# Six attentions on one core: the order of stages in six kinds of loop, and where SP issues the fold matrices

## The chip, the cores and the metric

The kernel runs on one core of one Trainium2 chip. The metric is the device time of one launch in microseconds (us), as the median of several runs. One more view, the profile, shows a single execution, instruction by instruction.

## The reference

Four transformer layers run one after another on `x` of shape (8, 512, 256), with a context of the same shape. Together they hold six attentions with 16 heads of 16 columns, and three feed-forward networks of width 1024:

```python
x = L0(x, ctx)   # attention 0: 64 wide causal window with slopes on x; attention 1: full, on ctx; FFN 0 (gelu)
x = L1(x, ctx)   # attention 2: causal on x, attention 3: full on ctx, both behind doubled projections; FFN 1 (gelu)
x = L2(x, ctx)   # attention 4: full, on the normalized ctx; FFN 2 (silu)
x = L3(x, ctx)   # attention 5: full, on ctx; layer norm
# each attention: softmax(q k^T * scale) v, then the output matrix, a residual and (mostly) a layer norm
```

## The kernel before

**Loops.** `LOOPS` (L110) lists 48 loops, one for each of 8 batch rows `b` and 6 attentions `a`. Batch rows go in pairs, and inside a pair the two rows alternate: (0,0), (1,0), (0,1), (1,1) and so on to (0,5), (1,5), then (2,0). `LOOP_NO` numbers them.

**Streams.** While one loop's attention runs, the tail of the loop before (output matrix, norms, feed-forward) and the start of the loop after (projections, first maxima) run beside it. `streams(j)` (L237) makes the lists: stream 0 is the attention's own 16 steps (`scores`, `values`, `sums`, `heads`, and `load` of the second half of the packed queries and keys), stream 1 its row maxima from head 6 on, stream 2 the work between, stream 3 what needs the context or a prefetched input. The first loop has a stream 4: `fold_stages` multiplies the doubled projections of attentions 2 and 3 into single matrices (six products in two halves, `fold`, with a `fold_bias` for each), then asks for later weights (`first_weights`) and makes five bias rows.

**The written order.** `MERGE` (L251) holds a string of digits for each kind of loop. Each digit takes the next stage from the stream of that number. The key is `first`, `last`, or the attention followed by the parity of the batch row. `plan()` walks the strings, and every engine goes through the resulting `PLAN` in the same order, doing its own share of each stage. An engine that waits therefore holds up everything behind it in the plan.

**How an attention's operands travel.** `project` makes q and k on TensorE (PE). ScalarE (ACT) writes the high bf16 part (L793), VectorE (DVE) the rest (L901), `middle` makes the middle part on ACT (L798) and the low part on GpSimd (POOL, L1027). SyncE (SP) sends each part to DRAM (L521) and, in `load`, fetches them back in the packed layout, twelve transfers of 128 KB for each half (L549). The `scores` matmuls (L693, with a mask at L696 or L698) need them. They also need minus the row maxima. PE computes scores for them from the high part (L670), with one head's queries left in by a mask made on POOL (L1021), and DVE takes the maxima (L911, L914) into `row_max`. For each group of four heads, `max_rows` transposes them (L923) and ACT issues an 8 KB write to DRAM (L811). `max_back` makes ACT wait until that write has landed, and then issues the read into the packed queries (L815). ACT then makes the exponentials (L829), PE the products with v (L718).

**y and out.** Norms go through the tile `y`: `rows` on PE (L765, L768) and DVE (L957), `stats` and `scale` on DVE with a power on POOL (L1033). After attention 5, `out` multiplies and adds on POOL (L1040, L1042), and SP stores `y`. A later `rows` stage that writes `y` waits for that store (`stored`, L952).

**The start.** SP issues, in this order: columns, the input of row 0, the squares of attention 0, tables, slopes, the input of row 1 (`load_inputs(1)`, 512 KB), and the fold matrices (1024, 512 and 1536 KB). Then it walks the plan. In the first `load` it also issues the context of rows 0 and 1, the bias rows and the squares of attention 1 (L553 to L556). At `first_weights` it issues the squares of attentions 2 to 5 at once and, when the last fold is done on PE, two weight loads of 1024 KB (L557 to L561).

Of the kernel before, what the change touches and what calls it, by code (L numbers as in the profile page):

```python
# [81 lines left out]
FOLDS = [f"{m}{a}" for a in (2, 3) for m in ("q", "k", "v")]  # L82
# [154 lines left out]
def streams(j):  # L237
# [6 lines left out]
    if j + 1 < len(LOOPS):  # L244
        (context if prefetched(*LOOPS[j + 1]) else between).extend(start_stages(*LOOPS[j + 1]))
        if not own(LOOPS[j + 1][1]):
# [2 lines left out]


MERGE = {  # L251
    "first": "244014414110101114111101101441111011011101141411101100114141011110110114110001410101112122222222"
           "2220020224424244422424444422040422220040400220024024222042202422004022000",
    "01": "011110111011101112301210111130111011101121122121011212103111011022111011211110011120010222222222"
           "0002222020000222002002202220220200202220002222222",
    "10": "012301230101210122222113112111020101101110112111010111010110010111011010111002100101101011010001"
           "10010012222220222002022202222020200202220200002222200220222200220",
    "11": "011100111101000021100111121012112220202101002211101011210101122220000210112121212221101201101001"
           "0110102011011211000212222220222222020222022022200220220000222002222202222022200",
    "20": "011100211102101111121221222101111200102111102101111211112111121111211101020002222202200102010210"  # L260
           "220110001012122222222222022202220020222000222200202222200220222200022000",
    "21": "023001121011011011011211221222101101120101011100101112301011012111100011121010101100101101011011"
           "312222022222020222020202220020202220220222200220222000222",
    "30": "012301230101210122222113112111020101101110112111010111010110010111011010111002100101101011010001"
# [4 lines left out]
    "40": "011010111011010101110102011111002200222200021010221101123303333312111201122330321011101221212122"  # L269
           "110202322010220022212332101022110101121100201222220222022222020200220220220000222020222022022222"  # L270
           "0220",
    "41": "012301230110201110101121111121111121111211100101120110111011010011101021102001100110010011000101"
           "2222233202220202220000222020022020200220200002222200220222200220",
    "50": "230101230110201110101121111121111121111211100101120110111011010011101022211020011001100100110001"
           "012222233202220202220000222020022020200220200002222200220222200220",
    "51": "230100121011101011211120131010111010101011101101110101011011010110001101101210101100101101010201"
           "333323200033333303030333030033330303330033033300033023233303323300",
    "00": "111230001211101101121110111111011122121011011110010111110101221030011200111002011101101113333023"
           "33333303033330333333333330003030033330030333300330",
    "last": "011101110101101011101011011110101110101110100210100010111212211001010101001001011011011101202001"  # L280
           "000200020000200020000200",
}
# [39 lines left out]
def program(nc, places, x_cols, c_cols, squares, folds_a, folds_b, w1, w2, cols, rows, tables, eye32,  # L322
            q_slopes, k_slopes, head_rows, q_dram, k_dram, r_dram, out):
    nc.disable_value_cache = True
    with ExitStack() as stack:
# [3 lines left out]
        def sem(name):  # L329
            return stack.enter_context(nc.semaphore(name))  # L330
# [41 lines left out]
        flat_hid, flat_w1, flat_w2 = (t[:].rearrange("p k n -> p (k n)") for t in (hid, w1s, w2s))  # L372
        fold_row = KT * D
        fold_w = FF // D
# [52 lines left out]
        folds_in = sem("folds_in")  # L427
# [52 lines left out]
        def _(sp):  # L480
            def cols_of(array, n):
                return array[n].rearrange("(k p) n -> p k n", p=P)
# [8 lines left out]
            def load_squares(a):  # L491

                first = SQ.index(f"o{a}") if a in FOLDED else SQ.index(f"q{a}")
                last = SQ.index(f"o{a}") + 1
                sp.dma_start(sq[:, first:last].rearrange("p s k n -> p (s k n)"),
                             squares[:, first * KT * D:last * KT * D]).then_inc(sq_in[a], 16)

            def load_inputs(s):

                sp.dma_start(xT[s][:], cols_of(x_cols, s)).then_inc(xT_in[s], 16)  # L500

            def load_context(s):

                sp.dma_start(cT[s][:], cols_of(c_cols, s)).then_inc(cT_in[s], 16)
# [6 lines left out]
            sp.dma_start(eye[:], eye32).then_inc(tabs_in, 16)  # L511
            sp.dma_start(packed["q"][MAXROW + 1:MAXROW + 1 + SLOPES], q_slopes).then_inc(tabs_in, 16)
            sp.dma_start(packed["k"][MAXROW + 1:MAXROW + 1 + SLOPES], k_slopes).then_inc(tabs_in, 16)
            load_inputs(1)
            sp.dma_start(flat_w1, folds_a[:, 0:fold_w * fold_row]).then_inc(folds_in, 16)
            sp.dma_start(flat_w2[:, 0:(len(FOLDS) - fold_w) * fold_row], folds_a[:, fold_w * fold_row:]).then_inc(folds_in, 16)
            sp.dma_start(flat_hid[:, 0:len(FOLDS) * fold_row], folds_b).then_inc(folds_in, 16)

            def send_part(b, a, m, w):

                sp.dma_start(in_dram[m][b % SLOTS, HML.index(w)].rearrange("(t p) n -> p t n", p=P), staged(b, m, w)) \  # L521
                    .then_inc(part_out[m, w], 16)

            for stage in PLAN:
# [11 lines left out]
                elif kind == "load":  # L536
# [7 lines left out]
                    for w in HML:  # L544
                        for m in "kq":
                            if half == 0:
                                sp.wait_ge(part_out[m, w], 16 * (j + 1))
                            for g in PART[m][w]:
                                sp.dma_start(packed[m][g:MAXROW:MAXROW // HD, at],  # L549
                                             in_dram[m][b % SLOTS, HML.index(w), half * P:(half + 1) * P]  # L550
                                             .rearrange("(h c) n -> c h n", c=HD)).then_inc(packed_in[half], 16)
                    if not j and not half:
                        load_context(0)  # L553
                        sp.dma_start(row[:], rows).then_inc(row_in, 16)
                        load_squares(1)
                        load_context(1)  # L556
# [623 lines left out]
```

## Time and profile before

| | |
|---|---|
| median of 3 runs | 3554.26 us (3553.37 to 3566.84) |
| the profiled execution | 3566.84 us, span 3565.0 us |
| busy: PE, DVE, ACT, POOL | 97%, 72%, 54%, 32% of the span |
| granted TensorE clock, mean of the span | 0.992 |
| chain that ended last | 83% PE, 11% DVE |

The profile gives each engine's busy time, what ended its idle times, and the chain of work that ended last. DMA queues are listed with the time from issue to landing. "Granted clock" is the share of full speed that TensorE was allowed: 1.00 is 2.4 GHz, 0.50 is 1.2 GHz.

### The profile page before, as it was taken

The page shows a single profiled execution, that of the slowest core. Times are in us where ns is not written, and L with a number is a line of the kernel's source. Part 1 is how long each engine was busy: PE and PEld are TensorE (multiplying, and loading weights), DVE is VectorE, ACT ScalarE, POOL GpSimd, SP SyncE. Part 2 cuts the span into 40 slices and gives each one's busy share as a digit, 9 for nine tenths or more (in the row PEclk, how much of TensorE's full clock was granted, in tenths as well). Part 3 has the DMA queues.
Part 4 walks back from the last instruction along what each step waited for, and adds up shares of the span by engine and source line. Part 5 has one row for each costly group of instructions (what it writes and reads, how often), then busy time and mean ns, then how long its engine had stood idle before and what let it go on. Part 6 is the DMA issues. An engine that isn't in the chain of part 4 may idle for free.

```text
span 3565.0 us, 53384 instructions
## 1 busy us (share of the span) xinstructions
PE 3446.8 (97%) x18672; PEld 1657.1 (46%) x18932; DVE 2572.8 (72%) x6523; ACT 1935.0 (54%) x2375; POOL 1143.4 (32%) x1049
## 2 busy tenths in 40 slices
PE   8899999999999999999999999999999999999998
PEld 5545544433454554443354455444335445445333
DVE  5766887756886588766778668777577956976667
ACT  2454565555555456555555545555564654655555
POOL 4322432222532242222253223222235322322222
PEclk9999999999999999999999999999999999999999
DMA  6311321223321231122332122112133312211211
GB/s 213 123 46 55 118 67 54 86 60 93 103 78 43 81 114 46 54 87 60 93 123 74 47 93 82 47 53 87 60 109 110 96 54 81 66 46 63 75 54 55
DMA packets 284317, 280.64 MB, mean 79 GB/s; under 512 B 49858, under 2 KB 275266, under 8 KB 280066
## 3 DMA queue, kind: packets, MB, share of 16 engines
q1 hardware_dynamic: 258324, 274.84, 24.0%
q10 hardware_dynamic: 25728, 2.36, 0.6%
q8 instruction: 154, 2.52, 0.3%
q14 instruction: 111, 0.91, 0.1%
HBM read 195.84 MB, written 81.26 MB: 78 GB/s over the span
## 4 chain that ended last, share of the span: by engine, by line
PE 83%; DVE 11%; issue 2%; ACT 2%; DMA 1%; SPq 1%; POOL 0%; another core or an unknown queue 0%; ACTq 0%; DVEq 0%
PE pv L718 14%; PE st L693 14%; PE mx L670 13%; PE mx L768 10%; PE mx L645 10%; PE st L731 9%; DVE row_max L911 5%; PE mx L742 4%; PE st L654 4%; PE mx L765 2%; PE st L778 2%; DVE mx L914 2%; ACT probs L829 1%; DVE turned L934 1%; DMA rows_of_max_dram<-max_rows 1%
## 5 line engine op out<-in xcount | busy, mean ns | idle before, releaser
L829 ACT ACTIVATE probs<-st 128x1024 f32<-128x1024 f32 (+1 forms) x1344 | 1266.6, 977 | 696.4 <-PE st L693 419.1
L911 DVE TENSOR_REDUCE row_max<-mx 128x1 bf16<-128x512 f32 x2048 | 1283.8, 684 | 216.3 <-PE mx L670 121.0
L1021 POOL TENSOR_TENSOR qm<-q_high,own_rows 128x512 bf16<-128x512 bf16 x768 | 797.3, 1044 | 1583.5 <-PE mx L670 1183.6
L670 PE MATMUL mx<-k_high,qm 128*128 128x512 bf16 (+4 forms) x2812 | 815.2, 342 | 44.7 <-DVE row_max L911 18.2
L693 PE MATMUL st<-q_packed,k_packed 97*128 97x512 bf16 (+2 forms) x3072 | 816.0, 346 | 27.3 <-DMA q_packed<-q_parts_dram 9.9
L718 PE MATMUL pv<-probs,va 128*32 128x512 f32 (+2 forms) x6144 | 701.8, 532 | 12.0 <-ACT probs L829 7.1
L670 PEld LDWEIGHTS mx<-k_high,qm 128*128 128x128 bf16 x3072 | 284.3, 98 | 604.0 <-DVE row_max L911 211.1
L914 DVE CUSTOM_DVE_ANT_0 mx<-mx,tab 128x192 f32<-128x192 f32 (+4 forms) x1024 | 400.9, 444 | 132.4 <-PE mx L670 118.7
L693 PEld LDWEIGHTS st<-q_packed,k_packed 97*128 97x128 bf16 (+1 forms) x3072 | 279.6, 98 | 435.0 <-ACT probs L829 149.8
L731 PE MATMUL st<-xT,w1s 128*128 128x512 f32 x768 | 342.9, 592 | 0.0
L957 DVE TENSOR_TENSOR y<-mx,row 128x256 f32<-128x256 f32 x224 | 94.8, 423 | 299.9 <-PE mx L768 297.2
L1033 POOL TENSOR_TENSOR rstd<-spread_of,m_half 128x2 f32<-128x2 f32 x144 | 100.5, 698 | 586.3 <-DVE spread_of L976 586.3
L718 PEld LDWEIGHTS pv<-probs,va 128*32 128x32 f32 x6144 | 126.1, 108 | 257.9 <-issue 201.8
L844 ACT ACTIVATE hid<-st,col 128x512 f32<-128x512 f32 x192 | 121.6, 685 | 224.3 <-PE st L731 224.3
L768 PE MATMUL mx<-w2s,hid 128*128 128x256 f32 x1024 | 231.6, 379 | 0.0
L731 PEld LDWEIGHTS st<-xT,w1s 128*128 128x128 f32 x768 | 144.7, 190 | 154.3 <-issue 145.4
L768 PEld LDWEIGHTS mx<-w2s,hid 128*128 128x128 f32 x1024 | 189.5, 190 | 23.1
L853 ACT ACTIVATE xT<-st,col 128x256 f32<-128x256 f32 x192 | 97.4, 562 | 174.2 <-PE st L778 123.6
L645 PE MATMUL mx<-xT,sq 128*128 128x512 f32 x352 | 163.9, 611 | 10.2 <-DMA sq<-squares_dram 8.0
L768 PE MATMUL mx<-sq,oT 128*128 128x256 f32 x640 | 166.9, 384 | 0.0
L838 ACT ACTIVATE sums<-pv 128x512 f32<-128x512 f32 x192 | 114.8, 598 | 86.2 <-PE pv L718 58.7
L914 DVE DVE_READ_ACCUMULATOR2_ANT row_max<- 128x1 bf16 x1024 | 147.9, 144 | 0.0
(88 smaller groups left out, 3141.5 us busy)
## 6 DMA issues: line engine op xcount, KB each, us to landing
k_packed<-k_parts_dram SPq DMA_DIRECT2D x576, 128.0 KB, 2.7
q_packed<-q_parts_dram SPq DMA_DIRECT2D x576, 128.0 KB, 2.7
q_parts_dram<-q_low SPq DMA_DIRECT2D x96, 256.0 KB, 2.2
k_parts_dram<-k_low SPq DMA_DIRECT2D x96, 256.0 KB, 2.5
q_parts_dram<-q_high SPq DMA_DIRECT2D x48, 256.0 KB, 2.1
k_parts_dram<-k_high SPq DMA_DIRECT2D x48, 256.0 KB, 2.3
w1s<-w_dram SPq DMA_DIRECT2D x12, 1024.0 KB, 5.1
w2s<-w_dram SPq DMA_DIRECT2D x12, 1024.0 KB, 7.6
```

The costliest lines, as they stand in the source:

```text
L645: mm = pe.matmul(bank, sqw(f"{m}{a}")[:, j, t * P:(t + 1) * P], src[:, j, :], start=(j == 0), stop=(j == KT - 1))
L654: mm = pe.matmul(pair[:, i // 2, i % 2 * D:(i % 2 + 1) * D], source(b, a)[:, j, i * P:(i + 1) * P], sqw(f"v{a}")[:, j, :], start=(j == 0), ...
L670: mm = pe.matmul(bank[:, 0:k1 - k0], qm[:, h % RING, i * P:(i + 1) * P], high["k"][s][:, t, k0:k1], start=True, stop=True)
L693: mm = pe.matmul(flat[:, c:c + w], kk[:, k * P:(k + 1) * P], qq[:, q0:q1], start=True, stop=(k_kind == FULL))
L718: mm = pe.matmul(pv[j * PAIR:(j + 1) * PAIR, q0:q1], va[s][:, k, at:at + PAIR], probs[:, step % 2, c:c + q1 - q0], start=(k == 0 and k_kin ...
L731: mm = pe.matmul(pair[:, e], w1s[:, j, at:at + P], xT[s][:, j, :], start=(j == 0), stop=(j == KT - 1))
L742: mm = pe.matmul(bank, weight[:, j, t * P:(t + 1) * P], src[:, j, :], start=(j == 0), stop=(j == count - 1))
L768: mm = pe.matmul(bank[:, 0:D], src[:, j, i * P:(i + 1) * P], weight[:, j, :], start=False, stop=(j == count - 1))
L829: act.activation(dst[:, :, 0:w], held["scores", b, a, n, e][:, :, 0:w], ACT.Exp, scale=ATT_SCALE[a]) \
L911: ins = dve.tensor_reduce(top, scores, AX_X, ALU.max, negate=True)
L914: ins = dve.tensor_tensor_reduce(scores, scores, hide[:, hide.shape[1] - (k1 - k0):hide.shape[1]], -1.0, 1e30, ALU.add, ALU.min, top)
L1021: pool.tensor_tensor(qm[:, h % RING], high["q"][s][:, h // HT], own_rows[:, h % HT:h % HT + 1].to_broadcast([P, TOK]), ALU.mult) \
```

## The change

Two things change. The strings of `MERGE` for the kinds `first`, `20`, `41`, `50`, `51` and `00` are replaced by other orders of the same stages. SP issues the fold matrices and the input of row 1, in that order, no longer at the start but inside the first `load`, behind its twelve packed transfers and ahead of the context. No instruction of any engine is added or removed.

In stages: in `first`, maxima of heads 6, 7 and part of 8 now stand first, then both projections of loop (1,0), then the second-half `load`, and only then the first scores. The folds stand at positions 63 to 120 of 169, where they began at 1. In `00`, eight maxima and the first two scores come ahead of `heads`, `project` q and `rows`. Two of the four `rows` of `a5` stand between the last row maxima and `project_v` (positions 88 and 89, before at 35 and 37). The two `out` stages move from positions 69 and 94 to 141 and 144 of 146. In `20` one maximum and `heads` move ahead of the first scores, and the feed-forward's stages are interleaved otherwise. In `41` two stages trade places with two at the front. In `50` the feed-forward, `project` q and the second `add` come later. In `51` the front and the tail are interleaved a little otherwise.

```diff
 MERGE = {
-    "first": "244014414110101114111101101441111011011101141411101100114141011110110114110001410101112122222222"
-           "2220020224424244422424444422040422220040400220024024222042202422004022000",
+    "first": "111111111111121201110011101111010011110101100110111000111100110414441411010110011122222222224442"
+           "4244422424442424424242444442204040004222400220024024222042202422004022000",
...
-    "20": "011100211102101111121221222101111200102111102101111211112111121111211101020002222202200102010210"
-           "220110001012122222222222022202220020222000222200202222200220222200022000",
+    "20": "011112002110110111121221222101111200102111102110101110110011121122200002121122122211020120101010"
+           "211010211212222222222220200022200222002220222002020222202002200222202200",
...
-    "00": "111230001211101101121110111111011122121011011110010111110101221030011200111002011101101113333023"
-           "33333303033330333333333330003030033330030333300330",
+    "00": "011111110111012322111011110111011101001111000111110110112001130101010110011101101113333322330233"
+           "33030333303333033330003330333303300033323300023223",
...
-            load_inputs(1)
-            sp.dma_start(flat_w1, folds_a[:, 0:fold_w * fold_row]).then_inc(folds_in, 16)
-            sp.dma_start(flat_w2[:, 0:(len(FOLDS) - fold_w) * fold_row], folds_a[:, fold_w * fold_row:]).then_inc(folds_in, 16)
-            sp.dma_start(flat_hid[:, 0:len(FOLDS) * fold_row], folds_b).then_inc(folds_in, 16)
-
...
                     if not j and not half:
+                        sp.dma_start(flat_w1, folds_a[:, 0:fold_w * fold_row]).then_inc(folds_in, 16)
+                        sp.dma_start(flat_w2[:, 0:(len(FOLDS) - fold_w) * fold_row], folds_a[:, fold_w * fold_row:]) \
+                            .then_inc(folds_in, 16)
+                        sp.dma_start(flat_hid[:, 0:len(FOLDS) * fold_row], folds_b).then_inc(folds_in, 16)
+                        load_inputs(1)
                         load_context(0)
                         sp.dma_start(row[:], rows).then_inc(row_in, 16)
                         load_squares(1)
```

## Rows read from the trace of the kernel before

**Rows 1.** The page, part 1: busy us, share of the span, instructions.

```profile
PE 3446.8 (97%) x18672; PEld 1657.1 (46%) x18932; DVE 2572.8 (72%) x6523; ACT 1935.0 (54%) x2375; POOL 1143.4 (32%) x1049
```

**Rows 2.** Windows: length, busy us of each engine, granted clock, DMA share, GB/s.

```profile
38.40:106.90 68.50, 53.79 (x459) 39.53 (x457) 37.94 (x180) 18.43 (x25) 20.84 (x18) 0.86 0.61 197
308.20:394.30 86.10, 83.77 (x498) 48.15 (x503) 51.43 (x186) 40.88 (x55) 23.68 (x22) 1.00 0.25 81
789.90:876.60 86.70, 86.17 (x356) 33.52 (x362) 52.66 (x90) 46.60 (x55) 20.90 (x18) 1.00 0.32 98
876.60:935.50 58.90, 57.52 (x320) 23.39 (x321) 50.36 (x132) 39.90 (x45) 27.44 (x24) 1.00 0.29 91
935.50:979.40 43.90, 39.74 (x388) 26.18 (x386) 34.44 (x165) 19.10 (x26) 27.16 (x24) 0.99 0.42 132
```

**Rows 3.** Waits of PE in the first loop, 38.4 to 106.9: us, times, longest.

```profile
PE pv L718 <- ACT probs L829: 5.6, 1, 5.6
PE st L693 <- DMA q_packed<-rows_of_max_dram: 5.6, 1, 5.6
PE mx L631 <- DMA sq<-squares_dram: 2.7, 1, 2.7
```

**Rows 4.** Waits of PE over the whole span: us in total, times, longest.

```profile
PE st L693 <- DMA q_packed<-q_parts_dram: 9.9, 3, 3.7
```

**Rows 5.** Windows as in Rows 2, of stretches at half clock.

```profile
49.80:60.00 10.20, 7.08 (x51) 5.26 (x51) 3.03 (x17) 2.22 (x3) 2.00 (x2) 0.50 0.24 49
1852.00:1858.80 6.80, 4.93 (x35) 3.63 (x36) 1.95 (x11) 1.62 (x2) 2.08 (x2) 0.50 0.64 197
2729.20:2732.60 3.40, 3.00 (x20) 2.84 (x21) 0.68 (x4) 0.81 (x1) 1.04 (x1) 0.50 0.67 206
```

**Rows 6.** DMA view of 4.62 to 6.6: issues, KB, us to landing.

```profile
hid<-folds_b_dram SPq DMA_DIRECT2D x1, 1536.0 KB, 18.8
...
xT<-x_cols_dram SPq DMA_DIRECT2D x1, 512.0 KB, 12.9
```

**Rows 7.** Timeline of SP, 23 to 48: start us, us, what it issues.

```profile
23.21 0.61 SPq L521 DMA_DIRECT2D k_parts_dram<-k_low  x1
26.34 1.97 SPq L549 DMA_DIRECT2D k_packed<-k_parts_dram  x3
...
33.48 0.60 SPq L549 DMA_DIRECT2D q_packed<-q_parts_dram  x1
```

**Rows 8.** Chain that ended last, 957 to 980: start us, us, what.

```profile
960.17 1.91 DMA rows_of_max_dram<-max_rows
...
962.35 1.07 ACT q_low L798
...
975.25 2.68 DMA q_packed<-q_parts_dram
```

**Rows 9.** Timeline of PE, 311.9 to 313.5: four matmuls of a `rows` stage.

```profile
312.53 1.03 PE L768 MATMUL mx<-sq,oT 128*128 128x256 f32 x4
```

**Rows 10.** Timeline of ACT, 66 to 68: the write of group 3's maxima.

```profile
67.46 0.53 ACTq L811 DMA_DIRECT2D rows_of_max_dram<-max_rows  x1
```

**Rows 11.** Chain that ended last, 20 to 110: start us, us, what.

```profile
27.84 6.07 PE mx L645 x8
...
66.48 3.52 PE mx L645 x8
...
75.91 0.89 PE mx L615 x4
...
77.77 0.79 PE mx L622 x8
...
89.25 13.28 DMA rows_of_max_dram<-max_rows
```

**Rows 12.** Timeline of SP, 70 to 103.

```profile
76.47 1.85 SPq L549 DMA_DIRECT2D k_packed<-k_parts_dram  x3
...
84.25 2.02 SPq L495 DMA_DIRECT2D sq<-squares_dram  x4
```

More of the change, by code:

```diff
@@ L271 @@
            "0220",
-    "41": "012301230110201110101121111121111121111211100101120110111011010011101021102001100110010011000101"
+    "41": "230101230110201110101121111121111121111211100101120110111011010011101021102001100110010011000101"
            "2222233202220202220000222020022020200220200002222200220222200220",
[L274 to L277, printed above, removed]
-    "00": "111230001211101101121110111111011122121011011110010111110101221030011200111002011101101113333023"
-           "33333303033330333333333330003030033330030333300330",
+    "50": "230101230110201110101101110011112111121111211112111011001121110001011010000111010110101000010212"
+           "200000222222332222020222020220220200022202000022222020202222022002",
+    "51": "112300012101101101010111211011121310010110110211101101010111011001110001011010101100101101100201"
+           "333323200303333303303303303300033033003330333000303232033333033230",
+    "00": "011111110111012322111011110111011101001111000111110110112001130101010110011101101113333322330233"
+           "33030333303333033330003330333303300033323300023223",
     "last": "011101110101101011101011011110101110101110100210100010111212211001010101001001011011011101202001"
```

## The prediction

> **What bounds the kernel now.** I read the page first. PE is busy for 3446.8 of 3565.0 us, so 118 us are idle [rows 1]. A new order of the same matmuls can win back only idle time, and time in which TensorE ran at half clock. I then cut the span into its 48 loops, at the first exponential of each, and read the busy time of PE in one loop of each changed kind. Length less busy time is PE's idle time: 14.7 us in `first` (68.5 less 53.8), 2.3 in `20`, 0.5 in `50` (`41` is like it), 1.4 in `51`, 4.2 in `00` [rows 2]. `first` occurs once, `20`, `41` and `50` four times, `51` and `00` three times. So the change works on about 14.7 + 9 + 4 + 4 + 13 = 45 us of idle time, and most of it is in two places.
>
> In `first`, three waits make up 13.9 of the 14.7 us, and the reader is to see that a DMA stands behind each: 5.6 for a read of row maxima, 2.7 for squares, 5.6 for an exponential [rows 3]. The chain shows what the exponential waited for. The 8 KB write of loop (1,0)'s first maxima was issued by ACT at 89.3 and took 13.3 us [rows 11]. ACT stands at `max_back` for all of it. SP had issued 4.5 MB of squares and weights from 84.3 on [rows 12].
>
> In `00`, PE waits three times, 9.9 us in all, for the packed queries of the next loop (2.6, 3.6 and 3.7) [rows 4]. The chain there: the write of group 3's maxima at 960.2, its landing, ACT's q_low at 962.4, POOL, twelve SP issues of which the last is at 975.3, and its landing 2.7 us later, 977.9 [rows 8]. PE was ready 2.6 us earlier, at 975.4.
>
> **`00`, three times.** I first asked whether moving `out` off POOL's path helps. It does not: POOL's q_low can't begin before ACT's q_low has ended at 963.4, and ACT begins it behind the landing of group 3's write [rows 8]. The new string keeps `max_rows`, `max_back` and `middle` q in that order, so the path from the write to the landing stays 17.8 us (977.9 less 960.2). In the second and third loop it is 1 us longer, since they stall 3.6 and 3.7. What changes is PE's work in that time. The new string puts two `rows` stages there that stood earlier. The four matmuls of one take 1.03 us [rows 9], about 1.1 with its transposes, so PE comes 2.2 us later. DVE gets some nine small operations more there (`rows`, `stats`, `scale`). At an estimated 0.4 us each that is 3.6 us, and DVE has room for them, being busy 34.4 of 43.9 us [rows 2]. So the three stalls shrink from 2.6, 3.6, 3.7 to about 0.4, 1.4, 1.5: 6.6 us gained, since the moved work is paid once in any order. With them goes half clock. After the second stall PE ran 4.93 busy us at 0.50, a loss of 2.5; after the third 3.00, a loss of 1.5 [rows 5]; I take 1.7 for the first. Short stalls of 1.4 us will keep part of it, so I take 2.5 of the 5.7. Against it, eight maxima at the loop's front make PE follow DVE, which I put at 0.6 us a loop. Sum: 6.6 + 2.5 - 1.8 = 7.3 us gained. Bounds: all stalls and losses gone, 15.6 gained; nothing gained and the store of `y` in the way (below), 7 lost.
>
> **`first`, once.** The queries' and keys' parts no longer queue behind 3.5 MB. SP has sent the last part at 23.2 + 0.6, so the packed loads begin at 23.9 and not at 26.3 [rows 7]. The last of the twelve is issued 7.1 us later, at 31.0, and lands at about 34.2 (2.7 us in [rows 8], 3.2 with a fuller queue). Folds and the input of row 1 come behind it. In the kernel before, that input took 12.9 us from issue to landing and the last fold, three issues later, 18.8 [rows 6]. At 0.5 us an issue [rows 12] that is 7.4 us for 3 MB. So the folds land at 41.6, and the 512 KB behind them at about 43.3. The bounds are 41, if they need not wait for the packed loads' end, and 48, if the 3.5 MB move as slowly as the 4.5 MB from 84.3 to 102.6 did, some 4 us a MB [rows 11, 12].
>
> The new string puts both projections of (1,0) ahead of the first scores, so PE stands still from about 29 to 43.3 and restarts at half clock, as it did at 27.8, where eight matmuls took 6.07 in place of 3.52 us [rows 11]. From there to the write of group 3's maxima took 39.6 us before (67.5 less 27.8) [rows 10, 11]. Of these, 5.6 are the wait for the maxima [rows 3], which goes, since their write now comes some 20 us before they are needed. The half clock behind it cost 7.08 / 2 = 3.5 [rows 5], and goes too. Moved in: one projection, 3.5, and one more score and value step, 1.1. Moved out: five fold halves of 0.9 and two pairs of biases of 0.8 [rows 11], 6.1, and nine maxima, 0.8. That leaves 28.2 us, so the write is issued at 71.5, 4.0 later than before.
>
> From this write a chain runs that PE does not set. Before: write at 67.5, packed loads from 76.5, squares from 84.3, and ACT's small write done at 89.3 + 13.3 = 102.6, when that backlog is through. The loop ended at 106.9, 4.3 later. Its order is kept, so each step moves by 4.0, or 3.5 because q_low no longer waits for the k projection. Taken by itself PE would be ready sooner: the folds it now still has to do cost it 4 us, but the 2.7 and 5.6 of waiting become one. So `first` ends at about 110.5 and not 106.9: 3.6 us lost. Bounds: if the small write is not held up, PE's own work sets the end. It is 71.5 plus 30.5 (39.4 before, from 67.5 to 106.9, less the stalls 2.7 and 5.6, less about 2 for half clock by the cost of the first stretch, less the projection 3.5, plus 5 for folds), 102.0, 5 gained. With the input at 48, 8.3 lost.
>
> On that small write the Trainium skill speaks, DMA: Bandwidth & Descriptors, section "Queues, rings and completion order": each DMA engine takes turns between the queues, packet by packet. By that rule ACT's 8 KB would not wait for SP's backlog. The trace disagrees: 13.3 us with the backlog, 1.9 without [rows 8, 11]. By the rule `first` would gain 5; by the rows it loses 3.6.
>
> **`20`, `41`, `50`, `51`.** PE is never short of work for long here [rows 2]. In `20`, `project` q stands farther behind its transposes, and 0.4 us of waiting each go: 1.5 for four. In `50` the q path to the next loop's packed loads gets shorter: from `project` q I count 9 us to the first issue and 10.3 to the landing, against about 27 us of PE work, so no wait. DVE has 52.7 us of work in 86.7. I take zero for these three, with 3 us either way.
>
> **Sum.** Against the profiled execution, 3566.8: -7.3 + 3.6 - 1.5 = -5.2, 3561.6. The median of the three runs is 12.6 lower than that execution. What made it slower I can't see, so I carry the difference over: 3554.3 - 5.2 = 3549.
>
> **The rivals.**
> *More gained (0.20).* In `00` the path itself shrinks, since the 512 KB store of `y` no longer shares the DMA engines with the parts and POOL has no `out` among its masks. With PE 2.2 us later the stalls then go entirely, and `first` is set by PE. For it: one of the three stalls is 1 us shorter than the others with the same work, so the path is not fixed. Against: the first 3 us of it are ACT's wait and q_low, which no `out` touches [rows 8]. 15.6 + 5 + 1.5 gained gives 3532.
> *The small write goes free (0.05).* `first` by PE alone, the rest as forecast: 3554.3 - 7.3 - 5 - 1.5 = 3540. The 13.3 us speak against it [rows 11]. The section of the Trainium skill cited above (DMA: Bandwidth & Descriptors) speaks for it.
> *Slower, by the store of y (0.13).* `out` of `a5` now ends on POOL after the loop's last maxima; store and landing follow, 2.6 + 0.4 + 3 us by my estimate, so about 5 us into the next loop. There DVE must write `y` for `a0` about 8 us after the start. SP also waits for this `out` ahead of the second-half `load`. It decides once `scale` comes more than 3 us late. At 2 us beyond that per loop, with no gain in `00`: 3554.3 + 3.6 - 1.5 + 6 = 3562.
> *It does nothing (0.12).* The stalls in `00` just move, `first` loses what `20` and the clock give: 3554, give or take 2.
>
> **The numbers.** The forecast has 0.50, and its own range is 3541 to 3558. All cases together: 3529 to 3566, which leaves out under 2 in 10. A measurement of this kernel can tell about 0.5% from no change, 17.8 us, so faster means under 3536.5 and slower above 3572. Faster gets most of the first rival and a small tail of others, 0.18. Slower gets the end of the store's case and a late input of row 1, 0.06. The rest, 0.76, is no change.
>
> **What the profile after would show.** PE idle from about 29 to 43, ended by the input of row 1, where before it worked. No wait for row maxima at about 47. The write of group 3 near 71.5, and ACT held at `max_back` until about 106. In `00`, stalls before the next loop's first scores of 0.4 to 1.5 us. In `20`, `41`, `50` and `51`, lengths within 1 us of before once moved stages are counted. The prediction is wrong if the input lands outside 41 to 48, if the maxima's write is not held up, if the stalls in `00` stay above 2.5, or if DVE waits for `stored` early in `01`.

## The result and the profile after

The change makes the kernel slower by about 20 us. The median after is 3576.6 us (3574.7 to 3578.39, 4 runs), before 3554.36 us (3553.37 to 3566.84, 4 runs), 22 us apart. The ratio is 1.0055, 95% interval 1.004 to 1.007. It is estimated from the runs as a whole and not from the two medians, and makes 19.6 us, between 14 and 25. In three later batches the kernel before had medians of 3557.6 to 3558.3. Each ratio of this document leaves out slow runs, of which there is one, of q1 below, at 12840.9 us. The forecast was 3549, with a range up to 3566. The profiled execution of after took 3585.01 us, span 3583.2, against 3565.0.

The page of after, part 1, answers to [rows 1]. PE is busy for 8.5 us longer though no matmul was added, DVE for 21 us.

```profile
PE 3455.3 (96%) x18669; PEld 1663.2 (46%) x18932; DVE 2593.9 (72%) x6523; ACT 1933.2 (54%) x2375; POOL 1140.2 (32%) x1049
```

I cut both spans at the first exponential of each loop. The end is 18.2 us later; of that the start has 2.0, the stretches from `10` to `20` of four pairs 2.5, those from `21` to `50` 1.2, and `51`, `00` and `01` at the three changes of pair 5.3, 2.8 and 4.6, together 12.7. The 2.5 understates what `20` lost, because the profiled execution of before was itself slow there: in the seven profiles below that keep the old `20`, the stretches from `10` to `20` are 2.7 to 5.9 us shorter than in it, in `11` and `20` (two of its four `20` take 87.7 and 87.1 us, the others 86.1). That is a part of the 12.6 us by which this execution lay above its median. Windows of after answer to [rows 2], in the same order of loops (`first`, `20`, `50`, `51`, `00`), with `01` behind them:

```profile
52.70:108.20 55.50, 49.38 (x462) 38.12 (x460) 35.83 (x167) 16.87 (x23) 18.35 (x16) 0.96 0.57 189
310.00:398.20 88.20, 84.44 (x497) 49.36 (x503) 52.56 (x185) 40.46 (x56) 23.46 (x22) 0.98 0.25 83
794.00:881.10 87.10, 86.80 (x357) 33.33 (x362) 53.67 (x91) 46.59 (x53) 20.72 (x18) 1.00 0.31 98
881.10:937.90 56.80, 55.54 (x312) 22.70 (x315) 48.24 (x132) 38.54 (x44) 27.42 (x25) 0.99 0.27 85
937.90:983.80 45.90, 41.63 (x390) 27.58 (x388) 38.80 (x157) 20.86 (x28) 22.29 (x20) 0.97 0.37 116
983.80:1041.50 57.70, 53.53 (x398) 31.09 (x402) 46.99 (x151) 23.01 (x33) 26.80 (x24) 0.91 0.38 120
```

I had no row of `01`, as its string does not change. Before it was:

```profile
979.40:1031.60 52.20, 49.85 (x397) 29.66 (x400) 44.47 (x143) 23.02 (x33) 22.14 (x20) 0.98 0.36 112
```

An unchanged loop grew by 5.5 us. Over `51`, `00` and `01` PE's busy time goes from 147.1 to 150.7 and its idle time from 7.9 to 9.7 us: 3.6 us of the 5.4 are longer busy time, which goes with the lower clock, and 1.8 are idle time. The stretches at half clock in after, as windows:

```profile
936.80:940.30 3.50, 3.50 (x21) 2.79 (x19) 2.49 (x14) 1.46 (x2) 3.04 (x4) 0.51 0.70 223
984.60:991.50 6.90, 5.86 (x29) 3.27 (x30) 5.34 (x24) 0.83 (x2) 6.01 (x6) 0.51 0.38 115
1035.80:1039.20 3.40, 3.40 (x5) 1.35 (x4) 2.79 (x6) 0.17 (x1) 0.56 (x1) 0.50 0.67 200
```

PE's waits over the whole span of after (us in total, times, longest) show what PE stood still for. The DMA wait of [rows 4] is gone. In its place are waits for row maxima, 26.4 us where before had 9.2, and for `oT`, 8.5 where before had 3.0.

```profile
PE mx L670 <- DVE row_max L914: 26.4, 37, 3.1
...
PE mx L645 <- DMA xT<-x_cols_dram: 12.6, 1, 12.6
PE mx L765 <- DVE oT L946: 8.5, 5, 3.0
```

**Where DVE was late.** The timelines of DVE, POOL and PE at the longest of these waits in the first `00` of after (start us, us, what, in brackets the wait before it):

```profile
967.20 0.71 DVE L946 STREAM_TRANSPOSE oT<-normal 128x512 f32<-128x512 f32 x1
967.84 3.81 DVE L982 TENSOR_SCALAR y<-y,moments,rstd 128x256 f32<-128x256 f32 x2
971.56 0.29 DVE L914 CUSTOM_DVE_ANT_0 mx<-mx,tab 128x128 f32<-128x128 f32 x1
```

```profile
967.23 2.13 POOL L1027 TENSOR_TENSOR q_low<-q_rest,q_low 128x1024 bf16<-128x1024 f32 x1 [3.01 <-ACT q_low L798]
969.32 2.17 POOL L1027 TENSOR_TENSOR k_low<-k_rest,k_low 128x1024 bf16<-128x1024 f32 x1
```

```profile
971.96 0.26 PE L670 MATMUL mx<-k_high,qm 128*128 128x192 bf16 x1 [2.56 <-DVE row_max L914]
```

The two operations of a `scale` stage take 3.81 us, where one usually takes 0.41. Their records overlap a little; the first runs 1.68 us and the second 2.21. In the other two `00` the pair is as slow, and PE's wait behind it is 3.08 and 2.92 us. The first ends at 969.52, 0.16 us after POOL's first subtraction (967.23 + 2.13), the second at 971.65, 0.16 after POOL's second. Some 15 us after it began it happens again, beside the two operations of `out`:

```profile
982.58 2.67 DVE L982 TENSOR_SCALAR y<-y,moments,rstd 128x256 f32<-128x256 f32 x2
```

```profile
982.49 1.26 POOL L1040 TENSOR_TENSOR y<-y,row 128x512 f32<-128x512 f32 x1
983.84 1.26 POOL L1042 TENSOR_TENSOR y<-y,row 128x512 f32<-128x512 f32 x1
```

Behind it PE waits 1.86 us, until 985.57, and half clock begins at 984.6, within this wait. A wait of 1.25 us ends just ahead of it, at 982.24, and has no collision in it: DVE does the tail of `heads` and then `stats` among the maxima there (a start of 980.52, 0.75 us for the two statistics, 0.25 for their aggregates). All `scale` operations of the program, by their line (min, median, max in ns), before and after:

```profile
L982 DVE TENSOR_SCALAR y<-y,moments,rstd x288: 373/408/1843, 122.9 to 3560.6; 128x256 f32<-128x256 f32 x144
```

```profile
L982 DVE TENSOR_SCALAR y<-y,moments,rstd x288: 374/406/2206, 124.8 to 3578.8; 128x256 f32<-128x256 f32 x144
```

Medians are alike; a few grew. Their total goes from 113.8 to 129.7 us: 16 of DVE's 21 us. The operations that take the row maxima, which read PSUM, are not slowed by the same operation on POOL. Before, DVE and POOL (two queries):

```profile
964.48 0.40 DVE L914 CUSTOM_DVE_ANT_0 mx<-mx,tab 128x192 f32<-128x192 f32 x1
```

```profile
963.48 2.13 POOL L1027 TENSOR_TENSOR q_low<-q_rest,q_low 128x1024 bf16<-128x1024 f32 x1 [0.38 <-ACT q_low L798]
```

**The start** came about much as forecast. PE's waits of after between 20 and 108.2, the chain there, and ACT's timeline, which answer to [rows 3, 10, 11]:

```profile
PE mx L645 <- DMA xT<-x_cols_dram: 12.6, 1, 12.6
PE pv L718 <- ACT probs L829: 4.3, 1, 4.3
```

```profile
32.91 9.94 DMA xT<-x_cols_dram
...
93.83 9.99 DMA rows_of_max_dram<-max_rows
```

```profile
70.19 0.53 ACTq L811 DMA_DIRECT2D rows_of_max_dram<-max_rows  x1
```

### The profile page after: what moved, and what is told of

It reads as the page before. It is cut to its first block, busy times and chain, and to the rows that moved or that the text cites. A ratio compares the mean times of both kernels' runs of the same rounds, so it can differ in the third digit from the quotient of the medians.

```text
span 3583.2 us, 53381 instructions
## 1 busy us (share of the span) xinstructions
PE 3455.3 (96%) x18669; PEld 1663.2 (46%) x18932; DVE 2593.9 (72%) x6523; ACT 1933.2 (54%) x2375; POOL 1140.2 (32%) x1049
## 4 chain that ended last, share of the span: by engine, by line
PE 82%; DVE 13%; issue 2%; ACT 1%; DMA 1%; POOL 0%; SPq 0%; another core or an unknown queue 0%; DVEq 0%; ACTq 0%
PE pv L718 14%; PE st L693 14%; PE mx L670 13%; PE mx L768 10%; PE mx L645 10%; PE st L731 9%; DVE row_max L911 5%; PE mx L742 4%; PE st L654 3%; DVE mx L914 3%; PE mx L765 2%; PE st L778 2%; DVE y L982 1%; DVE turned L934 1%; ACT probs L829 1%
## 5 line engine op out<-in xcount | busy, mean ns | idle before, releaser
L670 PE MATMUL mx<-k_high,qm 128*128 128x512 bf16 (+4 forms) x2809 | 818.3, 343 | 60.4 <-DVE row_max L914 26.4
L718 PE MATMUL pv<-probs,va 128*32 128x512 f32 (+2 forms) x6144 | 703.7, 532 | 13.3 <-ACT probs L829 5.5
L645 PE MATMUL mx<-xT,sq 128*128 128x512 f32 x352 | 161.5, 606 | 20.9 <-DMA xT<-x_cols_dram 12.6
```

What stands on the lines that cost most here:

```text
L645: mm = pe.matmul(bank, sqw(f"{m}{a}")[:, j, t * P:(t + 1) * P], src[:, j, :], start=(j == 0), stop=(j == KT - 1))
L670: mm = pe.matmul(bank[:, 0:k1 - k0], qm[:, h % RING, i * P:(i + 1) * P], high["k"][s][:, t, k0:k1], start=True, stop=True)
L718: mm = pe.matmul(pv[j * PAIR:(j + 1) * PAIR, q0:q1], va[s][:, k, at:at + PAIR], probs[:, step % 2, c:c + q1 - q0], start=(k == 0 and k_kin ...
```

## The experiments

Each batch ran beside the kernel before on its own chip; ratios are to that. Its median was 3557.61 us in the first batch (p), 3558.04 in the second (q), 3558.27 in the third (r). Between two batches the ratios are the better comparison, since the chips differ.

### The parts alone

Each kernel is the one before with one part of the change.

```diff
# p1: the new string of "first" and the new place of the fold and input transfers
# p2: the new string of "00"
# p3: the new string of "20"
# p4: the new strings of "41", "50", "51"
```

> The new `first` string and the moved start loads alone, all other strings as before. Theory (the loss sits in the strings of `00` and `20`): loop (1,0) begins 1.3 us later than before, as in the profile of the full change (108.2 against 106.9), and the time is 1 to 3 us over before. Rival (the start disturbs what follows, for instance the later loops' loads): 8 us or more over before.

> Only the string of `00` is new. Theory: the three pairs of loops `00` and `01` take as long as with the full change, so that this string alone carries most of the loss: 12 to 16 us over before, with six `scale` instructions of 1.3 to 2.2 us in place of 0.4 in each third of the run where DVE's L982 meets POOL's L1027 and L1040. Rival (the losses come from `51` before it handing over otherwise): 5 us or less.

> Only the string of `20` is new. Theory: PE waits 1.5 to 1.8 us for oT at the first `rows` stage of each of the four loops, and half clock follows in each: 3 to 6 us over before. Rival (the wait only takes the place of another of the same length): within 1 us.

> Only the strings of `41`, `50` and `51` are new. Both theories: within 2 us of before, since the lengths of `41` agree, and the 0.4 us that `50` gains in length and the 2.3 us that `51` loses are work handed to the next loop. If these strings matter by themselves: 4 us or more, either way.

| | median us | ratio, 95% interval | medians, us |
|---|---|---|---|
| p1, start | 3563.83 (3559.91 to 3566.03) | 1.0014 (1.0004 to 1.0023) | +6.2 |
| p2, `00` | 3567.33 (3564.82 to 3570.05) | 1.0025 (1.0016 to 1.0035) | +9.7 |
| p3, `20` | 3567.84 (3562.04 to 3571.76) | 1.0026 (1.0016 to 1.0035) | +10.2 |
| p4, `41`, `50`, `51` | 3560.81 (3555.26 to 3562.65) | 1.0006 (0.9996 to 1.0015) | +3.2 |

Three parts lose, and `00`, which was to gain 7.3, loses 9.7. The differences of medians add to 29 us, where the whole has 22; by the ratios it is 25 (0.71%) against 19.6, and the intervals are too wide to say that the parts are more than the whole. The expectations named the right places and missed the sizes. By the ratios p1 lost 5.0 us where 1 to 3 were expected, p2 8.9 where 12 to 16 were, and p3 9.2 where 3 to 6 were; the intervals just reach the expected ranges. p4 can't be told from no change. In p2 the first collision is there with the same 3.81 us, and PE's waits for the maxima in its first `00`, 932 to 981, are

```profile
PE mx L670 <- DVE row_max L914: 5.0, 3, 2.6
```

No wait for the packed queries is left in it. The three stretches `51`, `00`, `01` grow by 8.4 us in all, 12.7 in the full change. Time at half clock inside them adds up to 17 us in before, 37.5 in p2 and 41 in the full change.

In p3 the wait of 1.5 us for `oT` stands in each `20`, as expected, but half clock followed in two of the four only: those take 88.1 and 88.2 us, the other two 86.9 and 86.7.

### `00`: the collision taken away by moving DVE's operation

q1 is p2 with the first `scale` (half 0 of `a5`) at position 131 and not 93, behind POOL's subtractions. Position and order of all else stay.

```diff
# p2 -> q1
-    "00": "...101113333322330233"
-           "33030333303333033330003330333303300033323300023223",
+    "00": "...101113333322330333"
+           "30303333033330333300033303333033000233323300023223",
```

> The kernel with only the `00` string new, and in it the first `scale` of `a5` moved from position 93, where POOL runs its two 2.13 us operations, to position 131. Theory (a `scale` on DVE stands still while a wide POOL operation runs): the two instructions take 0.4 us each instead of 1.7 and 2.2, PE's idle time of 2.6 us near the middle of each `00` is gone, and the three `00` loops are 2 to 3 us shorter each; the time 6 us or more under that of the kernel with only `00` new. The second collision, with `out`, stays. Rival (DVE simply has too much to do there, or PE waits because rows were moved): `00` within 0.7 us of its length.

Measured: 3559.51 us, ratio 1.0004 (0.9994 to 1.0014), 7.8 us less than p2 (7.5 by the ratios), where 6 or more were expected. The three `00` take 44.5, 45.6 and 44.8 us and not 46.5, 47.0 and 45.2, less gain than the 2 to 3 us each that were expected; the unchanged `01` behind them take 53.0, 52.6 and 52.1 and not 55.6, 56.1 and 57.6. PE's waits in its first `00`, 932 to 985:

```profile
PE mx L670 <- DVE row_max L914: 2.0, 2, 1.3
PE st L693 <- DMA q_packed<-q_parts_dram: 1.1, 1, 1.1
```

The 2.56 is gone. The second collision still takes 2.67 us and the 1.25 ahead of it stays. What comes forward is the DMA stall, 1.1 us where before had 2.6 [rows 4]; in the three loops it is 1.1, 2.2 and 1.5. The forecast had 0.4, 1.4 and 1.5, so its term was of the right kind and 1.4 us too good; DVE's lateness had covered it.

q2 goes on: both `scale` and both `out` are placed anew, with the second `scale` ahead of both `out`.

```diff
# q1 -> q2
+    if tag == "a5":
+        yield "scale", b, tag, 1
+        yield last, b, tag, 0
+        yield last, b, tag, 1
+        return
-           "30303333033330333300033303333033000233323300023223",
+           "30303332303333033233000333033330330200332332300033",
```

> As the run before, and the second `scale` of `a5` now comes ahead of both `out` stages, with all of these stages some 10 positions earlier in `00` (in `51` and at the end of the program too, `scale` stands ahead of `out`). Theory: no `scale` instruction over 1.5 us in `00`, neither of the two waits of 1.3 and 1.9 us around the start of `01`, half clock after them gone: time at or under the kernel before, 0 to 8 us. Rival (the late `out` and its store hold up DVE or SP in `01`): waits of 2 us or more move into `01`, and the time stays 5 us or more over before.

Measured: 3560.11 us, 1.0007 (0.9998 to 1.0016). It is 7 us below p2, as q1 is, and not below q1. No `scale` is over 1.5 us, but in its first `00` three of them meet other work of POOL and take 0.92, 1.12 and 1.35 us. A `normal` (L943 in this kernel) beside an `out` takes 1.37 and not 0.42, and PE waits 1.85 and 2.68. That is a partial miss: one meeting was exchanged for others, here where POOL is busy for 27 of the 44 us of a `00` [rows 2].

r4 was to show the collision without the rest of the new string: the kernel before, with only the tail of `a5` placed near where the new `00` has it.

```diff
# before -> r4
-    "00": "...01221030011200111002011101101113333023"
-           "33333303033330333333333330003030033330030333300330",
+    "00": "...0101103001100111000111011011133330333233"
+           "33030333303333333333300030300333300303323300232230",
```

> The kernel before, and in `00` only `scale`, `stats`, `scale` and both `out` of `a5` moved to where the new string has them; `rows` and everything else stay. Theory (the collisions cost the time, not the moved `rows`): two `scale` instructions of 1.7 to 2.2 us while POOL makes the low parts, a PE wait of 2 us or more behind them, waits about 1.2 us around the start of `01`; 7 us or more over before. Rival (the moved `rows` or the new front of `00` cost it): within 3 us of before.

Measured: 3558.31 us, 1.0000 (0.9991 to 1.001). The first `scale` stage ran at 960.57, ahead of POOL's subtractions from 962.25 on, in 0.69 us for its two operations. So the collision that this run was made for didn't occur, and the run says nothing of it. Its level time fits the number of the rival, but `rows` and the new front aren't in it; q1 and r1 have both and are level with before too, so these don't cost the 9.7 us either. The second collision did occur, with 1.32 and 1.42 us for the two operations. PE's waits, 930 to 1032:

```profile
PE st L693 <- DMA q_packed<-q_parts_dram: 2.2, 1, 2.2
PE mx L670 <- DVE row_max L914: 2.0, 4, 1.3
```

The DMA stall behind it is 2.2 us where before had 2.6, and the kernel is level. So the second collision with its wait of 1.25 us, in front of a stall that remains, costs nothing that the runs can tell.

### `00`: the collision taken away by shortening POOL's operation

r1 has p2's string. POOL subtracts in two halves of the width; DVE's operations and their order are p2's.

```diff
-                    pool.tensor_tensor(low[m][:, 1], rest[m][:], low[m][:, 0], ALU.subtract) \
-                        .then_inc(*pool_step.mark(("l", b, a, m)))
+                    for t in range(KT):
+                        ins = pool.tensor_tensor(low[m][:, 1, t], rest[m][:, t], low[m][:, 0, t], ALU.subtract)
+                    ins.then_inc(*pool_step.mark(("l", b, a, m)))
```

> Only the string of `00` is new, and POOL makes each low part (L1027) in two operations of half the width. The order and all work of DVE stay. Theory (a `scale` waits until the POOL operation that is running has ended): the two `scale` instructions at the first collision take at most 1.2 us each in place of 1.7 and 2.2, PE's wait there falls from 2.6 to about 1 us, the others stay; 2 to 5 us less than with only `00` new (3567.3 where before ran 3557.6). Rival (DVE has too much to do there, whatever POOL does): durations and wait unchanged.

Measured: 3556.58 us, 0.9995 (0.9986 to 1.0004), 10.7 us less than p2, by the medians and by the ratios. The expectation had 2 to 5, so the collision costs more than twice what was thought even then. The edit acts in all 48 loops and not in `00` alone, but the profiles differ in `51`, `00` and `01` (11.9 us) and in the start (3.6, which varies, see below), and by under 1 us in all the rest. Timelines of DVE, POOL and PE of r1 at the same place:

```profile
957.20 1.87 DVE L982 TENSOR_SCALAR y<-y,moments,rstd 128x256 f32<-128x256 f32 x2
```

```profile
956.60 2.33 POOL L1028 TENSOR_TENSOR q_low<-q_rest,q_low 128x512 bf16<-128x512 f32 x2 [3.01 <-ACT q_low L798]
```

```profile
959.40 0.26 PE L670 MATMUL mx<-k_high,qm 128*128 128x192 bf16 x1 [0.63 <-DVE row_max L914]
```

The pair of `scale` takes 1.87 us and not 3.81, and PE waits 0.63 and not 2.56; in the other two `00` it is 1.15 each and not 3.09 and 3.04. This decides against the rival cause, that the new order simply gives DVE too much work at this place: DVE has the same work in r1. And PE's waits in its `00`, 928 to 975, again show the stall shrunk as forecast in kind:

```profile
PE mx L670 <- DVE row_max L914: 2.0, 3, 1.3
PE st L693 <- DMA q_packed<-q_parts_dram: 0.9, 1, 0.9
```

Both kinds of wait make 2.9 us, where p2 has 5.0. The stall is 0.9, 1.8 and 1.7 us in the three loops. Windows over `51`, `00` and `01` at all three changes of pair divide the rest (us, sums of three):

| | length | PE busy | PE idle | at half clock |
|---|---|---|---|---|
| before | 469.4 | 443.7 | 25.6 | 17 |
| p2 | 477.8 | 449.4 | 28.4 | 37.5 |
| q1 | 462.5 | 440.5 | 22.0 | 17 |
| r1 | 465.9 | 441.2 | 24.7 | 20.5 |
| after | 482.1 | 452.1 | 30.0 | 41 |

By the plan p2, q1 and r1 run the same matmuls in these windows; the time at half clock is read from the granted clock. p2 has 8.2 us more of busy time than r1 and 17 us more at half clock, half of which is 8.5, and 3.7 us more of idle time. So in these profiles some two thirds of the collision's cost is half clock and a third is waiting. No run held the clock fixed, so that the waits brought the half clock is argued: it came in p2 and after and went in q1 and r1, with the wait of 2.6 to 3.1 us.

### `20`: front or tail

q3 has the front of `20` as before, up to position 20, and the new order behind it.

```diff
# p3 -> q3
-    "20": "011112002110110111121221222101111200...",
+    "20": "011100211102101111121221222101111200...",
```

> Only the string of `20` is new, and only from position 20 on; its front is that of before. Theory (the loss of `20` is its front, where `rows` follows `heads` too closely): PE's wait for oT is gone, each `20` is 1.5 us or more shorter than in the run with the whole string, and the time is within 3 us of before. Rival (the interleaved feed-forward costs it): as slow as with the whole string, 5 us or more over before.

Measured: 3557.58 us, 0.9999 (0.999 to 1.0008), level with before, where p3 lost 10.2. PE's waits around `20`, 302 to 395, in p3 and then in q3:

```profile
PE mx L765 <- DVE oT L946: 1.5, 1, 1.5
PE mx L670 <- DVE row_max L914: 1.3, 3, 0.7
```

```profile
PE mx L670 <- DVE row_max L914: 1.3, 3, 0.7
PE st L693 <- issue: 0.4, 1, 0.4
```

Of the waits over half a microsecond only that for `oT` differs. The four `20` of q3 take 85.7, 85.9, 85.6 and 85.6 us, those of p3 88.1, 88.2, 86.9 and 86.7: 7.1 us. With the old string an undisturbed `20` takes 86.1 (p2, q1), so with the new tail a loop is some 0.4 us shorter, too little for the runs to tell. The timelines of DVE and PE of after show the chain:

```profile
310.72 0.42 DVE L938 TENSOR_TENSOR normal<-turned,rec 128x256 f32<-128x256 f32 x1
311.18 0.71 DVE L946 STREAM_TRANSPOSE oT<-normal 128x512 f32<-128x512 f32 x1
```

```profile
311.95 0.48 PE L765 MATMUL mx<-eye,xT 128*128 128x128 f32 x2 [1.46 <-DVE oT L946]
```

`heads` is four DVE operations long and `rows` needs its last. In the new string `011112002...` only the two `scores` halves stand between, and they don't cover it.

### The start: input of row 1 ahead of the folds

q4 is the full change with `load_inputs(1)` issued before the fold matrices.

```diff
                     if not j and not half:
+                        load_inputs(1)
                         sp.dma_start(flat_w1, folds_a[:, 0:fold_w * fold_row]).then_inc(folds_in, 16)
...
-                        load_inputs(1)
```

> The full change, but SP issues the input of row 1 ahead of the three fold loads. Theory (that input's landing sets the restart, and the chain behind it moves with it): the input lands at about 34.5 in place of 42.9, PE's wait of 12.6 us shrinks to about 4, and loop (1,0) starts at 101 to 103 in place of 108.2; 4 to 7 us less than the full change. Rival (the loads of squares and weights set the end of the first loop whatever PE does): (1,0) starts within 1.5 us of 108.2.

Measured: 3571.48 us, 1.0042 (1.0025 to 1.0059), 4 runs. The input lands at 36.4 and not 42.85, two microseconds later than I expected. PE's wait for it in q4:

```profile
PE mx L645 <- DMA xT<-x_cols_dram: 5.7, 1, 5.7
```

Loop (1,0) starts at 102.1 us, 6 earlier than after's 108.2. Profiles of other kernels repeat it: with the folds first it starts at 108.2 and 108.6 (after, p1), with the input first at 102.1, 103.0 and 100.9 (q4, r2, r3). What it is worth in the whole isn't shown: between the medians lie 5 us (3576.6 less 3571.48), with intervals that overlap. Before's own start is no fixed mark either: in kernels with the old start (1,0) begins anywhere from 102.2 to 106.9.

### The change with its faults mended

r2 is q4 with the front of `20` as before and the first `scale` of `00` at position 131. r3 keeps less: the kernel before, with q4's start and q3's `20`.

> The full change with three repairs: the input of row 1 ahead of the folds, the front of `20` as before, the first `scale` of `00` at position 131. Theory (the loss is the sum of the input's wait, the wait for oT and the first collision with its half clock): 3555 to 3562, level with before. Rival (something of the full change is still unexplained): 3567 or more.

> The kernel before with what helped: the new `first` string, folds and input of row 1 issued in the first `load` with the input first, and the new `20` string from position 20 on. Theory: loop (1,0) starts at about 102, `20` takes 85.7 us: 2 to 6 us faster than before. Rival (the start's gain is within what the start of the kernel before varies by): no difference.

Measured: r2 3553.92 us, 0.9987 (0.9978 to 0.9996); r3 3557.29 us, 0.9992 (0.9984 to 1.0001). r2 is a little faster than before, by 4.4 us on the same chip. That is under the 0.5% named in the prediction, but in a batch with 33 runs of before its interval leaves 1 out. r3 can't be told from before, though (1,0) starts at 100.9 and three of its `20` take 85.7 or less; the gain of 2 to 6 us that was expected isn't shown. Between q4 and r2 lie 19.6 us (1.0042 less 0.9987, times 3558; about 7 either way by the two intervals), for the front of `20` and one `scale` moved. That is as much as the whole loss of the full change, so most of it was in those two places.

## Why the prediction was wrong

**The step that failed.** "DVE gets some nine small operations more there (`rows`, `stats`, `scale`). At an estimated 0.4 us each that is 3.6 us, and DVE has room for them." The forecast gained 7.3 us in `00`, and p2 lost 9.7. The size came from operations that run beside nothing in their way, and the room from the average over a loop. The two `scale` beside POOL's subtractions took 3.81 us (after) instead of 0.8, at a place where PE was right behind the maxima, so PE stood 2.56 us. The small operations cost a further 1.25 us where `heads` and `stats` meet the maxima, so even undisturbed there was less room than the average said. q1 and r1 show it from both sides. The trace of before had the warning. [Rows 2] has POOL busy 27.16 of 43.9 us in `00`, and the longest `scale` of before took 1.84 us against a median of 0.41, which I looked up only after the result. I put no price on the stage that moves beside POOL's two longest operations.

**The DMA stall.** "So the three stalls shrink from 2.6, 3.6, 3.7 to about 0.4, 1.4, 1.5." Right in kind once the collision is away: 1.1, 2.2 and 1.5 in q1, 0.9, 1.8 and 1.7 in r1, together 4.7 and 4.3 where the forecast had 3.3 and before 9.9. In after it shrank to nothing, since PE came later still. So what was removed was replaced by waits on another engine, and idle time in `00` is the same as before (4.3 and 4.2 us, windows).

**The clock.** The forecast gave 2.5 us back. The measured sign is the other: waits for DVE of 2.56, 1.25 and 1.86 us stand within 17 us around the end of `00`, and `01` then runs 6.9 and 3.4 us at half clock. So it is at all three changes of pair. I had reckoned only with waits in the changed loop, and not looked at the unchanged loop behind it, which at the first change of pair loses as much as all three loops together (52.2 to 57.7 us).

**`20`.** "In `20`, `project` q stands farther behind its transposes, and 0.4 us of waiting each go: 1.5 for four." This is the second step that failed. A gain of 0.4 us a loop is there (85.7 in q3 against 86.1), but the front was priced at nothing: `heads` to `rows` was cut to two halves of scores. Alone it is about 10 us by the runs (p3 less q3, each against its own before), 7.1 by the profile.

**`first`.** The mechanism came out as forecast: the packed loads begin at 23.44 (forecast 23.9), the input of row 1 lands at 42.85 (43.3), the last fold at 41.5 (41.6), the write of group 3 is issued at 70.2 (71.5), the small write is held up again, 10.0 us, and (1,0) starts at 108.2 (110.5). The forecast's own rate of 7.4 us for 3 MB gives 42.8 for the input, not the 43.3 that it wrote. The loss is 1.3 us at that point and 2.0 a loop later, forecast 3.6. Alone by the runs it is 5.0 us by the ratio, 6.2 by the medians, with an interval of 1.4 to 8.2, which holds the 3.6. Since before's start varies by near 5 us, a forecast from one profiled execution could hardly do better; that 1.3 us of it show in the profile and 3.6 were forecast says little.

**`41`, `50`, `51`.** Taken as zero with 3 either way; +3.2 alone, which the runs can't tell from none.

**The rivals.** The store of `y` as the cause of a slower kernel did not come true: no wait for `stored` stands early in `01`. Its trigger was named, `scale` coming late, but put too far down the path: a late `scale` costs PE at once, through the maxima queued behind it on DVE. Its 3562 was the nearest of the single forecasts to 3576.6 only by luck. Full gain failed for the same reason. That the small write goes free did not come true either: it took 10.0 us.

**What stays open.** Why the clock falls a second time at 1035.8 behind small waits. In after and p2 it does so late in all three `01`, in before, with the same string of `01`, in one of three. Whether the parts alone add to more than the whole is not settled, nor whether q2's exchange of one meeting for others can be had cheaper. That the small write waits for SP's backlog was seen again, 8.4 to 10.7 us in the five profiles with the new start, and not tested by itself.

## What to carry to other kernels

Price a moved operation by what the other engines do at its new place. The slow examples of the same line are a warning and not a bound: before's longest `scale` took 1.84 us, after's 2.21; the length of the other engine's operation was the better guide. Read the loops behind the changed one too: here, behind waits of 2.56, 1.25 and 1.86 us, an unchanged loop ran 6.9 us at half clock. Before a consumer is moved up to its producer, count the other engine's chain between them. Asking for the small input that is needed next ahead of the big transfers started (1,0) 6 us earlier in the profiles.

## What the hardware showed

A `scale` (VectorE, f32, SBUF to SBUF, 128 x 256) takes 0.41 us alone, and 1.7 and 2.2 beside subtractions of 2.13 and 2.17 us on GpSimd; it ends 0.16 us behind them. The second `scale` lost again, to a subtraction that POOL began 0.12 us before it (969.32 against 971.65 less 2.21). Maxima that read PSUM kept their 0.40 us. The transpose into `oT`, SBUF to SBUF as well, kept its 0.71 us beside the first subtraction. `scale` isn't slowed in proportion: its time follows the length of the other engine's operation, and when that was split in two, the pair went from 3.81 to 1.87. A second operation of VectorE meets the same in both kernels: `normal` (L938), a `tensor_tensor` of two inputs in SBUF, has a median of 0.42 us, and in before three of 192 took 1.79 beside the same subtractions, each ending 0.28 us behind one. With the subtractions split (r1) these three took 0.81 to 0.82. The Trainium skill says why: SBUF — State Buffer, section "SBUF: two separate sides", has one pair of ports shared by the two engines as an exclusive lock, which whoever starts first holds for the whole instruction, and VectorE: DVE Perf Modes, section "Mode 2×_2P — use both read ports for one tensor", has f32 `tensor_scalar` from SBUF as one that uses both ports and reads of PSUM as one that can't. The trace agrees in what it can show: in both collisions at 967.84 POOL had begun first, `scale` ends just behind it, and reads of PSUM go on. It shows no ports, and not why `scale` needs only 0.16 us behind POOL's end where it takes 0.41 alone.

An 8 KB write of ACT's queue took 10.0 us while SP's transfers were under way, as in [rows 11] with 13.3, against 1.9 in a quiet stretch [rows 8]. That these transfers hold it up is inferred from the times alone.
